# A graph-network layer on one core: layer two one group later, messages two groups further ahead

## The chip, the core and the metric

The kernel runs on one core of a Trainium2 chip, in a single launch. The metric is device time in microseconds; the time of the kernel before is 476.75 us, the median of three runs (476.61 to 477.19). TensorE (PE) does the matrix products and the transposes, VectorE (DVE) and ScalarE (ACT) the elementwise work, GpSimd (POOL) issues the gathers, SyncE (SP) all other transfers.

## The reference, cut to what matters

```python
# x (50000, 128); src, dst (25000,), dst sorted; edge_attr (25000, 128); W1 (128, 256); W2 (256, 128)
msg = relu(x[src] + edge_attr)
agg = segment_sum(msg, dst, num_segments=50000)
h = x + agg
h = relu(relu(h @ W1 + b1) @ W2 + b2)
out = layernorm(x + h)            # over the 128 features, no scale, no shift
```

## The kernel before

**Tiling.** The 50000 nodes are cut into 98 groups: 97 of 512 nodes (T = 4 tiles of 128) and a last one of 336. The edges are sorted by target, so the edges of a group lie in three windows of 128 edges, each for a third of its nodes (K = 3).

**What a group takes.** SP loads its x (`x_sb`) and its three windows of edge_attr (`pre_msg`); POOL gathers x[src] (`x_src`), three indirect transfers. DVE adds the two (`add_edge_attr`, L568). ACT takes the relu rounded to a short form, `msg_hi` (`high_part`, L718), and DVE what the rounding left, `msg_lo` (`low_part`, L575). DVE also writes `sel`, a matrix of ones and zeros that says which edge belongs to which node (`select`, L551). PE turns x (`turn_x`, L812, four transposes) and adds the messages on top in the same PSUM bank (`sum_messages`, L834, six products); ACT copies that to `hT` (`copy_hT`, L724). Layer one is `hidden_sum` on PE (L859, two products of 128x512) and `hidden` on ACT (L730, bias and relu into `h1T`); layer two is `output_sum` on PE (L867, eight products). DVE adds the bias (`add_bias`, L589), takes the relu and adds x (`add_x`, L601), and computes mean and variance (L608, L617); ACT takes the root (`deviation`, L735), DVE the reciprocal and the shift (L623, L628), ACT scales the four tiles (`normalize`, L749), SP stores.

**What sets the order.** The order on every engine is written out by hand, and each engine runs its own list strictly in order, waiting on semaphores. In the steady part, iteration g holds:
- PE: hidden_sum(g), turn_x(g+1), sum_messages(g+1), output_sum(g)
- ACT: hidden(g), deviation(g-2), copy_hT(g+1), normalize(g-3) with high_part(g+2) in its middle
- DVE: add_bias(g), low_part(g+2), add_x(g), reciprocal(g-2), statistics(g), shifts(g-2), select(g+3), aggregate(g), add_edge_attr(g+3)
- SP: x of group g+5, edge_attr of group g+5, the store of group g-4
- POOL: the gathers of group g, once `hT` of group g-3 is copied (GATHER_AHEAD = 3)

PSUM has eight banks: one for `hT_ps`, two for layer one (`h1T_ps`), two for layer two (`h2_ps`), two of the preparation (`prep_ps`) and a spare one. After group 3 the preparation's banks hold only one thing more, the sum of some flags (`sums_ps`, in `prep_ps[0]`), which say whether the windows are wide enough for the data. `sum_flags` writes it on PE in iteration CHECKED = 30, and `set_general` (L312) reads it on DVE at the end of iteration 31.

Of the kernel before, what the change touches and what calls it, by code (L numbers as in the profile page):

```python
# [8 lines left out]
ACT = mybir.ActivationFunctionType  # L9
AX_X = mybir.AxisListType.X  # L10
# [5 lines left out]
T = 4  # L16
# [17 lines left out]
ROWS = 125  # L34
CHECKED = 30
FAR = float(1 << 20)


EB, XB, ZB, YB, SB = 6, 6, 6, 4, 4
X_FIRST, X_AHEAD = 2, 5  # L40
GATHER_AHEAD = 3
ACT_TILES = 1
EA_FIRST, EA_AHEAD = 2, 5

# [118 lines left out]
def prepare(nc, x, edge_attr, dst, pairs, w1, b1, w2, b2, c, sb, sem):  # L163
# [9 lines left out]
    prep_ps = c["prep_ps"]  # L173
# [135 lines left out]
    def set_general(dve):  # L309

        dve.wait_ge(flags_summed, 1)
        nc.vector.reduce_max(c["general"][:, :], sums_ps, AX_X)  # L312

# [101 lines left out]
def main_path(nc, x, pairs, edge_attr, out, c, sb, sem, checks):  # L415
# [22 lines left out]
    hT = sb("hT", [128, T, 128])  # L438
    h1T = sb("h1T", [128, HC, T, 128])
    h2 = sb("h2", [128, 2, T, D])  # L440
# [18 lines left out]
    h2_summed = sem("h2_summed")  # L459
    h2_ready = sem("h2_ready")  # L460
    z_ready = sem("z_ready")
    stats_ready = sem("stats_ready")
# [8 lines left out]
    last_y_pool_ready = sem("last_y_pool_ready")  # L471

    def inside(g):

        return 0 <= g < GROUPS

    def main_sync(sp):
# [68 lines left out]
    def main_vector(dve):  # L546
# [8 lines left out]
        def edge_attr_there(g):  # L555

            dve.wait_ge(ea_loaded[g % EB], loads_to(g % EB, g, 0, c))
# [52 lines left out]

        def aggregate(g):
            p = partitions(g, c)
            dve.wait_ge(stats_ready, g + 1)
            for t in range(tiles(g, c)):
                if t == 1 and g >= 1 and inside(g + 3):
                    edge_attr_there(g + 3)
                last = nc.vector.bn_aggr(mean_var[0:p, g % SB, t, :], stats[0:p, g % SB, t, :])  # L617
            last.then_inc(var_ready, 1)
# [49 lines left out]
        statistics(1)  # L668
        select(4)
        aggregate(1)  # L670
        add_edge_attr(4)
        for g in range(2, LAST):
            add_bias(g)
            if inside(g + 2):
                low_part(g + 2)
            add_x(g)
            if inside(g - 2):
                reciprocal(g - 2)
            if g == LAST - 1:
                reciprocal(LAST - 2)  # L680
            statistics(g)
            if inside(g - 2):
                shifts(g - 2)
            if g == LAST - 1:
                shifts(LAST - 2)
            z_free(g + 1)
            if inside(g + 3):
                select(g + 3)
            aggregate(g)
            if inside(g + 3):  # L690
                add_edge_attr(g + 3)
            if g == CHECKED + 1:
                checks["set_general"](dve)
        add_bias(LAST)
# [13 lines left out]
    def main_scalar(act):  # L708
# [17 lines left out]
        def hidden(g, h):  # L726

            p, n = partitions(g, c), tiles(g, c)
            act.wait_ge(h1_summed, g * HC + h + 1)
            nc.scalar.activation(h1T[:, h, 0:n, 0:p], h1T_ps[h][:, 0:n, 0:p], ACT.Relu, bias=b1_sb[:, h:h + 1]).then_inc(h1_ready, 1)  # L730

# [43 lines left out]
        high_part(4)  # L775
        for g in range(3, LAST):
            for h in range(HC):
                hidden(g, h)
            if inside(g - 2):
                deviation(g - 2)  # L780
            if inside(g + 1):
                copy_hT(g + 1)
            for t in range(T):
                if inside(g - 3):
                    last = normalize(g - 3, t)
                if t == 1 and inside(g + 2):
                    high_part(g + 2)
            if inside(g - 3):
                last.then_inc(y_ready, 1)
        deviation(LAST - 2)  # L790
# [13 lines left out]
    def main_tensor(pe):  # L804
# [48 lines left out]
        def hidden_sum(g):  # L853
            p, n = partitions(g, c), tiles(g, c)
            pe.wait_ge(hT_copied, g + 1)
            for h in range(HC):
                if h == 1 and inside(g - 2):
                    pe.wait_ge(h2_ready, g - 1)
                nc.tensor.matmul(h1T_ps[h][:, 0:n, 0:p], w1_sb[:, h * 128:(h + 1) * 128], hT[:, 0:n, 0:p],  # L859
                                 start=True, stop=True).then_inc(h1_summed, 1)  # L860

        def output_sum(g, h):

            p = partitions(g, c)
            pe.wait_ge(h1_ready, g * HC + h + 1)
            for t in range(tiles(g, c)):
                last = nc.tensor.matmul(h2_ps[g % 2][0:p, t, :], h1T[:, h, t, 0:p], w2_sb[:, h, :],  # L867
                                        start=(h == 0 and t == 0), stop=(h == HC - 1), skip_group_check=True)
            if h == HC - 1:
                last.then_inc(h2_summed, 1)  # L870
# [31 lines left out]
        for g in (1, 2):  # L902
# [9 lines left out]
            output_sum(g, 1)  # L912
        for g in range(3, GROUPS):
            hidden_sum(g)
            if inside(g + 1):
                turn_x(g + 1)
                sum_messages(g + 1)
            if g == CHECKED:
                checks["sum_flags"](pe)
            for h in range(HC):  # L920
                output_sum(g, h)

# [370 lines left out]
```

## Time and profile before

| | |
|---|---|
| time, median of 3 runs | 476.75 us (476.61 to 477.19) |
| profiled execution, span from the first to the last instruction | 508.3 us |
| what the profile shows around that span | nothing that is timed |
| PE busy | 469.2 us (92%) |
| DVE busy | 409.9 us (81%) |
| ACT busy | 399.9 us (79%) |
| POOL busy | 320.8 us (63%) |
| mean granted TensorE clock | 0.991 of full speed |
| moved by DMA | 90.89 MB, 179 GB/s on average |

The profiled execution is 31.6 us longer than the median of the runs. A busy engine in the table is one that an instruction occupies; for PE the ends are modelled, so the start of the next row tells more than the length of a row. A wait that ends on "issue" or "remote" is one whose releaser the profile does not show.

### The profile page before, as it was taken

Reading aid. Unit: us, or ns where it says so; the run is one execution under the profiler, and the core shown is the slowest. Engines: PE = TensorE matmul, PEld = TensorE weight load, DVE = VectorE, ACT = ScalarE, POOL = GpSimd, SP = SyncE. Lnnn points to the kernel's source line nnn. Section 1 sums busy time; section 2 is a strip of 40 time slices with the busy share of each in tenths; the row PEclk is TensorE's granted clock in tenths of the full one; section 3 lists DMA queues with packets and bytes.
Section 4 is the critical chain, followed back from the end, with each engine's and each line's share of the span. In section 5 each row is a group of like instructions: output and inputs, shape, how many; then the busy total and the mean of one; then the engine's idle time right before and its main releaser. Section 6 shows DMA issues by size and latency. Waiting matters only on the chain.

```text
span 508.3 us, 9923 instructions
## 1 busy us (share of the span) xinstructions
PE 469.2 (92%) x2959; PEld 360.2 (71%) x2959; DVE 409.9 (81%) x1539; ACT 399.9 (79%) x881; POOL 320.8 (63%) x315
## 2 busy tenths in 40 slices
PE   5879999999989999989998989989899989989994
PEld 3647777676776777767786767767677867767773
DVE  6567879788797887977887877878778878878885
ACT  2328988797888898877887877878778878878885
POOL 7566766666756676666766656656566666666713
PEclk9979999999999999999999999999999999999999
DMA  5644656655656566655666656657556666656613
GB/s 134 168 135 155 193 185 201 196 175 184 195 173 190 183 206 203 177 174 177 195 199 181 192 173 184 186 172 204 170 183 186 202 182 182 203 173 188 218 58 117
DMA packets 81930, 90.89 MB, mean 179 GB/s; under 512 B 13841, under 2 KB 52372, under 8 KB 81876
## 3 DMA queue, kind: packets, MB, share of 16 engines
q1 hardware_dynamic: 71874, 70.80, 43.3%
q0 software_dynamic: 9728, 19.46, 16.6%
q8 instruction: 23, 0.38, 0.3%
q14 instruction: 31, 0.25, 0.1%
q10 hardware_dynamic: 274, 0.00, 0.0%
HBM read 64.61 MB, written 25.60 MB: 177 GB/s over the span
## 4 chain that ended last, share of the span: by engine, by line
PE 87%; issue 5%; ACT 3%; DVE 2%; another core or an unknown queue 2%; DMA 1%; POOL 0%; SPq 0%; DVEq 0%
PE h_ps L867 33%; PE h1T_ps L859 32%; PE hT_ps L834 13%; PE hT_ps L812 8%; ACT h1T L730 1%; ACT y L749 1%; ACT hT L724 1%; DMA dst_next<-in_dst_dram 1%; ACT msg_hi L718 0%; DVE stats L608 0%; DVE z L601 0%; DVE h L589 0%; DVE before_in_row L288 0%; DVE row_holds L358 0%
## 5 line engine op out<-in xcount | busy, mean ns | idle before, releaser
L109 POOL DMA_INDIRECT x_src<-in_x_dram,src_of x287 | 306.5, 1068 | 165.7 <-ACT hT L724 91.6
L867 PE MATMUL h_ps<-w_sb,h1T 128*128 128x128 f32 x1564 | 195.3, 278 | 3.2 <-ACT h1T L730 3.1
L867 PEld LDWEIGHTS h_ps<-w_sb,h1T 128*128 128x128 f32 x1564 | 183.7, 193 | 5.0 <-ACT h1T L730 4.9
L859 PE MATMUL h1T_ps<-hT,w_sb 128*128 128x512 f32 x392 | 185.7, 596 | 1.6 <-ACT hT L724 1.1
L730 ACT ACTIVATE h1T<-h1T_ps,b_sb 128x512 f32<-128x512 f32 x196 | 128.8, 680 | 55.6 <-PE h1T_ps L859 30.8
L749 ACT ACTIVATE y<-z,shift,rstd 128x128 f32<-128x128 f32 x382 | 165.6, 481 | 1.4 <-DVE shift L628 1.3
L589 DVE TENSOR_TENSOR h<-h_ps,b_sb 128x512 f32<-128x512 f32 x98 | 67.4, 688 | 81.9 <-remote 37.6
L859 PEld LDWEIGHTS h1T_ps<-hT,w_sb 128*128 128x128 f32 x392 | 67.5, 192 | 49.3 <-issue 47.7
L834 PE MATMUL hT_ps<-sel,msg_hi 128*128 128x168 f32 (+1 forms) x281 | 72.9, 293 | 20.8 <-issue 20.8
L608 DVE BATCH_NORM_STATS2 stats<-z 128x6 f32<-128x128 f32 x391 | 85.3, 281 | 0.0
L812 PEld LDWEIGHTS hT_ps<-ident,x_sb 128*128 128x128 f32 (+1 forms) x375 | 46.9, 141 | 50.0 <-issue 49.6
L724 ACT ACTIVATE hT<-hT_ps 128x512 f32<-128x512 f32 (+1 forms) x95 | 56.5, 595 | 21.5 <-PE hT_ps L834 17.5
L834 PEld LDWEIGHTS hT_ps<-sel,msg_hi 128*128 128x128 f32 x281 | 53.7, 191 | 26.3 <-issue 26.3
L834 PE MATMUL hT_ps<-sel,msg_lo 128*128 128x168 f32 (+1 forms) x281 | 67.4, 275 | 0.0
L601 DVE SCALAR_TENSOR_TENSOR z<-h,x_sb 128x512 f32<-128x512 f32 x98 | 66.8, 682 | 0.1
L551 DVE TENSOR_TENSOR sel<-node_in_range,dst_of 128x528 fp32r<-128x528 f32 x95 | 66.6, 701 | 0.0
L718 ACT ACTIVATE msg_hi<-pre_msg 128x384 fp32r<-128x384 f32 (+1 forms) x99 | 50.9, 514 | 17.5 <-issue 14.0
L575 DVE SCALAR_TENSOR_TENSOR msg_lo<-pre_msg,msg_hi 128x384 fp32r<-128x384 f32 (+1 forms) x99 | 54.0, 546 | 3.3 <-ACT msg_hi L718 2.2
L812 PE MATMUL hT_ps<-ident,x_sb 128*128 128x128 f32 (+1 forms) x375 | 56.3, 272 | 0.0
L568 DVE TENSOR_TENSOR pre_msg<-pre_msg,x_src 128x384 f32<-128x384 f32 (+2 forms) x101 | 51.7, 512 | 4.6 <-issue 2.9
L834 PEld LDWEIGHTS hT_ps<-sel,msg_lo 128*128 128x128 f32 x281 | 53.9, 192 | 0.0
L617 DVE BATCH_NORM_AGGREGATE mean_var<-stats 128x2 f32<-128x6 f32 x391 | 36.4, 155 | 0.1
(115 smaller groups left out, 121.2 us busy)
## 6 DMA issues: line engine op xcount, KB each, us to landing
x_sb<-in_x_dram SPq DMA_DIRECT2D x97, 256.0 KB
out_dram<-y SPq DMA_DIRECT2D x97, 256.0 KB
pre_msg<-in_edge_attr_dram SPq DMA_DIRECT2D x292, 64.0 KB
x_src<-in_x_dram,src_of POOLq DMA_INDIRECT x287
w_sb<-in_w_dram SPq DMA_DIRECT2D x2, 128.0 KB
x_sb<-in_x_dram SPq DMA_DIRECT2D x1, 168.0 KB
out_dram<-y SPq DMA_DIRECT2D x1, 168.0 KB
dst_rows<-in_dst_dram SPq DMA_DIRECT2D x1, 97.7 KB
```

The costliest lines, as they stand in the source:

```text
L109: nc.gpsimd.indirect_dma_start(out=c["x_src"][:, g % EB, k, :], out_offset=None, in_=x, in_offset=bass.IndirectOffsetOnAxis(ap=c["src_of"] ...
L551: nc.vector.tensor_tensor(sel[:, g % EB, 0:n, 0:width], in_range[:, :, :].to_broadcast([128, n, width]), dst_of[:, g:g + 1, 0:n].rearrange ...
L589: nc.vector.tensor_tensor(h2[0:p, g % 2, 0:n, :], h2_ps[g % 2][0:p, 0:n, :], b2_sb[0:p, :, :].to_broadcast([p, n, D]), ALU.add).then_inc(h ...
L601: nc.vector.scalar_tensor_tensor(z[0:p, g % ZB, 0:n, :], h2[0:p, g % 2, 0:n, :], 0.0, x_sb[0:p, g % XB, 0:n, :], ALU.max, ALU.add).then_in ...
L608: last = nc.vector.bn_stats(stats[0:p, g % SB, t, :], z[0:p, g % ZB, t, :])
L724: nc.scalar.activation(hT[:, 0:n, 0:p], sum_bank(g)[:, 0:n, 0:p], ACT.Copy).then_inc(hT_copied, 1)
L730: nc.scalar.activation(h1T[:, h, 0:n, 0:p], h1T_ps[h][:, 0:n, 0:p], ACT.Relu, bias=b1_sb[:, h:h + 1]).then_inc(h1_ready, 1)
L749: return nc.scalar.activation(y[0:p, g % YB, t, :], z[0:p, g % ZB, t, :], ACT.Identity, bias=shift[0:p, g % SB, t:t + 1], scale=rstd[0:p, ...
L812: nc.tensor.matmul(sum_bank(g)[:, t, 0:p], x_sb[0:p, g % XB, t, :], ident[0:p, 0:p], is_transpose=True, start=(t == 0), stop=False, skip_g ...
L834: last = nc.tensor.matmul(sum_bank(g)[:, 0:n, p0:p1], part[:, g % EB, k, :], cols, start=False, stop=final, skip_group_check=True)
L859: nc.tensor.matmul(h1T_ps[h][:, 0:n, 0:p], w1_sb[:, h * 128:(h + 1) * 128], hT[:, 0:n, 0:p], start=True, stop=True).then_inc(h1_summed, 1)
L867: last = nc.tensor.matmul(h2_ps[g % 2][0:p, t, :], h1T[:, h, t, 0:p], w2_sb[:, h, :], start=(h == 0 and t == 0), stop=(h == HC - 1), skip_ ...
```

## The change

Three things are moved, each by a constant or by the written order.

**PE and ACT.** From group LAG + 1 = 7 to UNLAG = 92, iteration g of PE does output_sum(g-1) in the place of output_sum(g). Iteration 6 has no output_sum, iteration 92 has two. `h1T` gets a second buffer, and layer one of every second group from 7 on writes to the two banks of the preparation (`hidden_bank`). For these banks to be free, the flags are summed in iteration 4 in place of 30 (CHECKED), and PE waits for set_general, a new semaphore, ahead of hidden_sum(7). On ACT, copy_hT(g+1) comes ahead of hidden(g), and deviation and normalize are of one group further back; at group 92 the old order returns, with one more deviation and one more normalize.

**DVE.** At group 6 DVE does low_part(8), select(9), add_edge_attr(9), select(10), low_part(9) and add_edge_attr(10) in one go. From there iteration g does select(g+5), low_part(g+4) and add_edge_attr(g+5) in the place of g+3, g+2 and g+3.

**Buffers and queues.** The buffers of messages, gathers and selections go from 6 to 8, those of x from 6 to 7. POOL's gathers of group g wait for hT of group g-5. SP loads edge_attr 6 groups ahead.

```diff
@@ -32,15 +32,18 @@
 LW = max(LP0[k + 1] - LP0[k] for k in range(LK))
 
 ROWS = 125
-CHECKED = 30
+CHECKED = 4
 FAR = float(1 << 20)
 
 
-EB, XB, ZB, YB, SB = 6, 6, 6, 4, 4
+EB, XB, ZB, YB, SB = 8, 7, 6, 4, 4
 X_FIRST, X_AHEAD = 2, 5
-GATHER_AHEAD = 3
+GATHER_AHEAD = 5
 ACT_TILES = 1
-EA_FIRST, EA_AHEAD = 2, 5
+EA_FIRST, EA_AHEAD = 2, 6
+
+LAG = 6
+UNLAG_BACK = 5
 
 FIRST_CHUNKS = 5
 SECOND = {1: (0, P0[1]), 2: (0, 128), 3: (0, 128), 4: (P0[2], 128)}
@@ -309,7 +312,7 @@
     def set_general(dve):
 
         dve.wait_ge(flags_summed, 1)
-        nc.vector.reduce_max(c["general"][:, :], sums_ps, AX_X)
+        return nc.vector.reduce_max(c["general"][:, :], sums_ps, AX_X)
 
     def find_ends(pe):
 
@@ -436,7 +439,7 @@
     msg_lo = sb("msg_lo", [128, EB, K, D], FP32R)
     msg_whole = sb("msg_whole", [128, len(WHOLE), D])
     hT = sb("hT", [128, T, 128])
-    h1T = sb("h1T", [128, HC, T, 128])
+    h1T = sb("h1T", [128, 2, HC, T, 128])
     h2 = sb("h2", [128, 2, T, D])
     z = sb("z", [128, ZB, T, D])
     y = sb("y", [128, YB, T, D])
@@ -458,6 +461,7 @@
     h1_ready = sem("h1_ready")
     h2_summed = sem("h2_summed")
     h2_ready = sem("h2_ready")
+    general_set = sem("general_set")
     z_ready = sem("z_ready")
     stats_ready = sem("stats_ready")
     var_ready = sem("var_ready")
@@ -470,9 +474,15 @@
     last_y_dve_ready = sem("last_y_dve_ready")
     last_y_pool_ready = sem("last_y_pool_ready")
 
+    UNLAG = LAST - UNLAG_BACK
+
     def inside(g):
 
         return 0 <= g < GROUPS
+
+    def hidden_bank(g, h):
+
+        return c["prep_ps"][h].rearrange("p (t n) -> p t n", t=T) if g > LAG and (g - LAG) % 2 else h1T_ps[h]
 
     def main_sync(sp):
         def load_x(g):
@@ -608,12 +618,12 @@
                 last = nc.vector.bn_stats(stats[0:p, g % SB, t, :], z[0:p, g % ZB, t, :])
             last.then_inc(stats_ready, 1)
 
-        def aggregate(g):
+        def aggregate(g, ahead=None):
             p = partitions(g, c)
             dve.wait_ge(stats_ready, g + 1)
             for t in range(tiles(g, c)):
-                if t == 1 and g >= 1 and inside(g + 3):
-                    edge_attr_there(g + 3)
+                if t == 1 and ahead is not None and inside(ahead):
+                    edge_attr_there(ahead)
                 last = nc.vector.bn_aggr(mean_var[0:p, g % SB, t, :], stats[0:p, g % SB, t, :])
             last.then_inc(var_ready, 1)
 
@@ -667,11 +677,25 @@
         add_x(1)
         statistics(1)
         select(4)
-        aggregate(1)
+        aggregate(1, 4)
         add_edge_attr(4)
         for g in range(2, LAST):
+            if g == LAG:
+                low_part(g + 2)
+                select(g + 3)
+                edge_attr_there(g + 3)
+                add_edge_attr(g + 3)
+                select(g + 4)
+                low_part(g + 3)
+                edge_attr_there(g + 4)
+                add_edge_attr(g + 4)
+            lagged = g >= LAG
+            ahead = g + (5 if lagged else 3)
             add_bias(g)
-            if inside(g + 2):
+            if lagged:
+                if inside(ahead):
+                    select(ahead)
+            else:
                 low_part(g + 2)
             add_x(g)
             if inside(g - 2):
@@ -684,13 +708,15 @@
             if g == LAST - 1:
                 shifts(LAST - 2)
             z_free(g + 1)
-            if inside(g + 3):
-                select(g + 3)
-            aggregate(g)
-            if inside(g + 3):
-                add_edge_attr(g + 3)
+            if not lagged:
+                select(ahead)
+            elif inside(g + 4):
+                low_part(g + 4)
+            aggregate(g, ahead)
+            if inside(ahead):
+                add_edge_attr(ahead)
             if g == CHECKED + 1:
-                checks["set_general"](dve)
+                checks["set_general"](dve).then_inc(general_set, 1)
         add_bias(LAST)
         add_x(LAST)
         reciprocal(LAST - 1)
@@ -727,7 +753,7 @@
 
             p, n = partitions(g, c), tiles(g, c)
             act.wait_ge(h1_summed, g * HC + h + 1)
-            nc.scalar.activation(h1T[:, h, 0:n, 0:p], h1T_ps[h][:, 0:n, 0:p], ACT.Relu, bias=b1_sb[:, h:h + 1]).then_inc(h1_ready, 1)
+            nc.scalar.activation(h1T[:, g % 2, h, 0:n, 0:p], hidden_bank(g, h)[:, 0:n, 0:p], ACT.Relu, bias=b1_sb[:, h:h + 1]).then_inc(h1_ready, 1)
 
         def deviation(g):
             p, n = partitions(g, c), tiles(g, c)
@@ -773,20 +799,45 @@
         deviation(0)
         copy_hT(3)
         high_part(4)
-        for g in range(3, LAST):
+        def normalize_all(g, between=None):
+            for t in range(T):
+                last = normalize(g, t)
+                if t == 1 and between is not None and inside(between):
+                    high_part(between)
+            last.then_inc(y_ready, 1)
+
+        for g in range(3, LAG):
             for h in range(HC):
                 hidden(g, h)
-            if inside(g - 2):
-                deviation(g - 2)
-            if inside(g + 1):
-                copy_hT(g + 1)
-            for t in range(T):
-                if inside(g - 3):
-                    last = normalize(g - 3, t)
-                if t == 1 and inside(g + 2):
-                    high_part(g + 2)
+            deviation(g - 2)
+            copy_hT(g + 1)
             if inside(g - 3):
-                last.then_inc(y_ready, 1)
+                normalize_all(g - 3, g + 2)
+            else:
+                high_part(g + 2)
+        copy_hT(LAG + 1)
+        high_part(LAG + 2)
+        for h in range(HC):
+            hidden(LAG, h)
+        high_part(LAG + 3)
+        for g in range(LAG + 1, UNLAG):
+            copy_hT(g + 1)
+            for h in range(HC):
+                hidden(g, h)
+            deviation(g - 3)
+            normalize_all(g - 4, g + 3)
+        for g in range(UNLAG, LAST):
+            for h in range(HC):
+                hidden(g, h)
+            if g == UNLAG:
+                deviation(g - 3)
+            deviation(g - 2)
+            copy_hT(g + 1)
+            if g == UNLAG:
+                normalize_all(g - 4)
+            if inside(g + 3):
+                high_part(g + 3)
+            normalize_all(g - 3)
         deviation(LAST - 2)
         for h in range(HC):
             hidden(LAST, h)
@@ -855,8 +906,8 @@
             pe.wait_ge(hT_copied, g + 1)
             for h in range(HC):
                 if h == 1 and inside(g - 2):
-                    pe.wait_ge(h2_ready, g - 1)
-                nc.tensor.matmul(h1T_ps[h][:, 0:n, 0:p], w1_sb[:, h * 128:(h + 1) * 128], hT[:, 0:n, 0:p],
+                    pe.wait_ge(h2_ready, g - 2 if LAG < g <= UNLAG else g - 1)
+                nc.tensor.matmul(hidden_bank(g, h)[:, 0:n, 0:p], w1_sb[:, h * 128:(h + 1) * 128], hT[:, 0:n, 0:p],
                                  start=True, stop=True).then_inc(h1_summed, 1)
 
         def output_sum(g, h):
@@ -864,7 +915,7 @@
             p = partitions(g, c)
             pe.wait_ge(h1_ready, g * HC + h + 1)
             for t in range(tiles(g, c)):
-                last = nc.tensor.matmul(h2_ps[g % 2][0:p, t, :], h1T[:, h, t, 0:p], w2_sb[:, h, :],
+                last = nc.tensor.matmul(h2_ps[g % 2][0:p, t, :], h1T[:, g % 2, h, t, 0:p], w2_sb[:, h, :],
                                         start=(h == 0 and t == 0), stop=(h == HC - 1), skip_group_check=True)
             if h == HC - 1:
                 last.then_inc(h2_summed, 1)
@@ -911,14 +962,22 @@
             sum_messages(g + 1)
             output_sum(g, 1)
         for g in range(3, GROUPS):
+            if g == LAG + 1:
+                pe.wait_ge(general_set, 1)
             hidden_sum(g)
             if inside(g + 1):
                 turn_x(g + 1)
                 sum_messages(g + 1)
             if g == CHECKED:
                 checks["sum_flags"](pe)
-            for h in range(HC):
-                output_sum(g, h)
+            if LAG < g <= UNLAG:
+                for h in range(HC):
+                    output_sum(g - 1, h)
+            if g == UNLAG:
+                pe.wait_ge(h2_ready, g - 1)
+            if g < LAG or g >= UNLAG:
+                for h in range(HC):
+                    output_sum(g, h)
 
     return dict(sync=main_sync, gpsimd=main_gpsimd, vector=main_vector, scalar=main_scalar, tensor=main_tensor)
```

The instructions of PE where the two orders part; `h1T_ps0` and `prep_ps0` are banks of layer one, `h2_ps` of layer two. Before, the end of iteration 6 and the head of iteration 7:

```order
L834 MATMUL hT_ps<-sel,msg_lo 128x4x42
L867 MATMUL h2_ps0<-w2_sb,h1T 128x128 [waits h1_ready]
L867 MATMUL h2_ps0<-w2_sb,h1T 128x128 x3
L867 MATMUL h2_ps0<-w2_sb,h1T 128x128 [waits h1_ready]
L867 MATMUL h2_ps0<-w2_sb,h1T 128x128 x3
L859 MATMUL h1T_ps0<-hT,w1_sb 128x512 [waits hT_copied]
L859 MATMUL h1T_ps1<-hT,w1_sb 128x512 [waits h2_ready]
```

The same place of PE in the changed kernel:

```order
L885 MATMUL hT_ps<-sel,msg_hi 128x4x42
L885 MATMUL hT_ps<-sel,msg_lo 128x4x42
L910 MATMUL prep_ps0<-hT,w1_sb 128x512 [waits hT_copied,general_set]
L910 MATMUL prep_ps1<-hT,w1_sb 128x512 [waits h2_ready]
L863 MATMUL hT_ps<-ident,x_sb 128x128 [waits x_loaded1]
```

The eight products of layer two of group 6 have gone from here to the end of iteration 7, and hidden_sum(7) waits for one semaphore more.

DVE at the end of iteration 5 and the head of iteration 6, before:

```order
L568 TENSOR_TENSOR pre_msg<-pre_msg,x_src 128x384 [waits xsrc_loaded2]
L589 TENSOR_TENSOR h2<-h2_ps0,b2_sb 128x512 [waits h2_summed]
L575 SCALAR_TENSOR_TENSOR msg_lo<-pre_msg,msg_hi 128x384 [waits msg_hi_ready]
L601 SCALAR_TENSOR_TENSOR z<-h2,x_sb 128x512 [waits h2_ready]
L623 RECIPROCAL rstd<-std 128x4 [waits std_ready]
```

The same place of DVE in the changed kernel:

```order
L578 TENSOR_TENSOR pre_msg<-pre_msg,x_src 128x384 [waits xsrc_loaded0]
L315 TENSOR_REDUCE general<-prep_ps0 1x1 [waits flags_summed]
L585 SCALAR_TENSOR_TENSOR msg_lo<-pre_msg,msg_hi 128x384 [waits msg_hi_ready]
L561 TENSOR_TENSOR sel<-node_in_range,dst_of 128x528
L578 TENSOR_TENSOR pre_msg<-pre_msg,x_src 128x384 [waits xsrc_loaded1,ea_loaded1]
L561 TENSOR_TENSOR sel<-node_in_range,dst_of 128x528
L585 SCALAR_TENSOR_TENSOR msg_lo<-pre_msg,msg_hi 128x384 [waits msg_hi_ready]
L578 TENSOR_TENSOR pre_msg<-pre_msg,x_src 128x384 [waits xsrc_loaded2,ea_loaded2]
L599 TENSOR_TENSOR h2<-h2_ps0,b2_sb 128x512 [waits h2_summed]
L561 TENSOR_TENSOR sel<-node_in_range,dst_of 128x528
```

The reduction that PE waits for stands behind the whole of iteration 5, and the work that brings DVE two groups ahead stands between it and the bias of group 6.

ACT in iteration 6 before, a round of the steady part:

```order
L730 ACTIVATE h1T<-h1T_ps0,b1_sb 128x512 [waits h1_summed]
L730 ACTIVATE h1T<-h1T_ps1,b1_sb 128x512 [waits h1_summed]
L735 ACTIVATE std<-mean_var,eps_col 128x4 [waits var_ready]
L724 ACTIVATE hT<-hT_ps 128x512 [waits hT_summed]
L749 ACTIVATE y<-z,shift,rstd 128x128 [waits shift_ready]
L749 ACTIVATE y<-z,shift,rstd 128x128
L718 ACTIVATE msg_hi<-pre_msg 128x384 [waits sum_ready]
```

ACT in iteration 7 of the changed kernel, the first such round in the new order:

```order
L750 ACTIVATE hT<-hT_ps 128x512 [waits hT_summed]
L756 ACTIVATE h1T<-prep_ps0,b1_sb 128x512 [waits h1_summed]
L756 ACTIVATE h1T<-prep_ps1,b1_sb 128x512 [waits h1_summed]
L761 ACTIVATE std<-mean_var,eps_col 128x4 [waits var_ready]
L775 ACTIVATE y<-z,shift,rstd 128x128 [waits shift_ready]
L775 ACTIVATE y<-z,shift,rstd 128x128
L744 ACTIVATE msg_hi<-pre_msg 128x384 [waits sum_ready]
```

The copy of the next group's `hT` has moved ahead of the relu of this group's layer one.

## Rows read from the trace of the kernel before

**Rows 1.** The chain that ended last: shares of the span by engine.
```profile
PE 87%; issue 5%; ACT 3%; DVE 2%; another core or an unknown queue 2%; DMA 1%; POOL 0%; SPq 0%; DVEq 0%
```
**Rows 2.** Timeline of PE: start us, us, engine line op out<-in xcount [idle before <-releaser].
```profile
252.29 1.88 PE L859 MATMUL h1T_ps<-hT,w_sb 128*128 128x512 f32 x4
...
254.37 0.33 PE L834 MATMUL hT_ps<-sel,msg_hi 128*128 128x176 f32 x1
...
255.09 1.98 PE L867 MATMUL h_ps<-w_sb,h1T 128*128 128x128 f32 x16
256.90 0.59 PE L859 MATMUL h1T_ps<-hT,w_sb 128*128 128x512 f32 x1
```
**Rows 3.** Timeline of DVE, the same stretch.
```profile
252.52 0.68 DVE L589 TENSOR_TENSOR h<-h_ps,b_sb 128x512 f32<-128x512 f32 x1
253.19 0.56 DVE L575 SCALAR_TENSOR_TENSOR msg_lo<-pre_msg,msg_hi 128x384 fp32r<-128x384 f32 x1
253.66 0.68 DVE L601 SCALAR_TENSOR_TENSOR z<-h,x_sb 128x512 f32<-128x512 f32 x1
...
255.17 0.14 DVE L628 SCALAR_TENSOR_TENSOR shift<-mean_var,rstd 128x4 f32<-128x4 f32 x1
255.23 0.70 DVE L551 TENSOR_TENSOR sel<-node_in_range,dst_of 128x528 fp32r<-128x528 f32 x1
255.85 0.37 DVE L617 BATCH_NORM_AGGREGATE mean_var<-stats 128x2 f32<-128x6 f32 x4
256.14 0.52 DVE L568 TENSOR_TENSOR pre_msg<-pre_msg,x_src 128x384 f32<-128x384 f32 x1
```
**Rows 4.** Timeline of ACT, the same stretch.
```profile
252.63 0.53 ACT L718 ACTIVATE msg_hi<-pre_msg 128x384 fp32r<-128x384 f32 x1 [0.47 <-issue]
253.06 0.86 ACT L749 ACTIVATE y<-z,shift,rstd 128x128 f32<-128x128 f32 x2
253.83 1.24 ACT L730 ACTIVATE h1T<-h1T_ps,b_sb 128x512 f32<-128x512 f32 x2
254.97 0.29 ACT L735 ACTIVATE std<-mean_var,eps_col 128x4 f32<-128x4 f32 x1
255.29 0.60 ACT L724 ACTIVATE hT<-hT_ps 128x512 f32<-128x512 f32 x1
255.78 0.87 ACT L749 ACTIVATE y<-z,shift,rstd 128x128 f32<-128x128 f32 x2
```
**Rows 5.** Waits of PE: total us, times, longest us.
```profile
PE hT_ps L834 <- issue: 20.8, 23, 1.4
```
**Rows 6.** Timeline of PE, one pause.
```profile
222.48 0.60 PE L812 MATMUL hT_ps<-ident,x_sb 128*128 128x128 f32 x4
224.49 0.35 PE L834 MATMUL hT_ps<-sel,msg_hi 128*128 128x176 f32 x1 [1.41 <-issue]
```
**Rows 7.** Timeline of DVE, the same pause.
```profile
220.00 0.53 DVE L568 TENSOR_TENSOR pre_msg<-pre_msg,x_src 128x384 f32<-128x384 f32 x1
223.28 0.69 DVE L589 TENSOR_TENSOR h<-h_ps,b_sb 128x512 f32<-128x512 f32 x1 [2.76 <-issue]
```
**Rows 8.** Timeline of PE: layer one of group 4 and of group 96.
```profile
41.92 1.88 PE L859 MATMUL h1T_ps<-hT,w_sb 128*128 128x512 f32 x4
...
494.25 1.88 PE L859 MATMUL h1T_ps<-hT,w_sb 128*128 128x512 f32 x4
```
**Rows 9.** Timeline of groups 2 and 3, PE and ACT.
```profile
30.60 1.16 PE L867 MATMUL h_ps<-w_sb,h1T 128*128 128x128 f32 x8 [2.01 <-ACT h1T L730]
...
35.02 0.60 ACT L724 ACTIVATE hT<-prep_ps 128x512 f32<-128x512 f32 x1 [3.41 <-remote]
...
35.67 3.52 PE L859 MATMUL h1T_ps<-hT,w_sb 128*128 128x512 f32 x4 [1.09 <-ACT hT L724]
```
**Rows 10.** Busy times of 20 to 40 us: length, PE, PEld, DVE, ACT, POOL, granted clock, DMA.
```profile
20.00:40.00 20.00, 16.44 (x81) 11.59 (x79) 13.97 (x48) 6.95 (x15) 13.46 (x13) 0.83 0.57 168
```
**Rows 11.** The reduction of the flags on DVE: duration in ns, start.
```profile
L312 DVE TENSOR_REDUCE general<-prep_ps x1: 147/147/147, 182.9 to 182.9; 1x1 int32<-1x9 f32 x1
```
**Rows 12.** Timeline of POOL, two gathers of one group.
```profile
252.98 0.94 POOL L109 DMA_INDIRECT x_src<-in_x_dram,src_of  x1 [0.30 <-issue]
254.23 0.95 POOL L109 DMA_INDIRECT x_src<-in_x_dram,src_of  x1 [0.30 <-issue]
```

## The prediction

> **What bounds the kernel now.** I read the chain of waits first: PE holds 87% of it [rows 1]. Then the timeline of PE over one group, to see how full it is. H(g) is the start of hidden_sum(g) below. From one H to the next it is 256.90 - 252.29 = 4.61 us [rows 2]: sum_messages begins at H + 2.08, output_sum at H + 2.80, the next group at H + 4.61, and no row in between has idle time ahead of it. So in such a group PE has nothing left to wait for, and what the change may win must come from groups that are longer.
>
> These exist in the profiled execution. From H(4) at 41.92 to H(96) at 494.25 [rows 8] there are 92 groups, 452.3 us, where 92 x 4.61 makes 424.1. That leaves 28.2 us. The waits of PE show them as 23 pauses ahead of sum_messages [rows 5]. One of them: the transposes begin at 222.48, the first message product at 224.49, 2.01 us later where 0.36 would do [rows 2, 6]. DVE says why: it had nothing to do from 220.53 on and began add_bias only at 223.28, after 2.76 us of idle time [rows 7], though by PE's rows output_sum had ended long before. PE's signal came late, low_part stood behind add_bias, and PE waited for low_part.
>
> Are these pauses in the timed runs? The profiled execution takes 508.3 us (nothing that is timed lies around its span), the runs 476.75: 31.6 less. The pauses make 28.2, a further one ahead of 30.60 makes 2.0 [rows 9], and hidden_sum(3) ran in 3.52 us where others take 1.88 [rows 2, 9], since the granted clock was 0.83 in that stretch, so at 1.2 GHz for a part of it [rows 10]: 1.6. Together 31.8. So I take it that the timed runs have next to none of them. How much could they have? ACT idled another 3.41 us before the copy of group 3 [rows 9], also for a late signal; if that too belongs to the profiled execution alone, 5 us or so of the timed runs are unexplained, and may be pauses or something around the span. Bounds for what the change can win back: 0 and 5 us. I take 0, since the sum closes.
>
> The Trainium skill, page "Runtime: NRT & Kernel Launch", section "The ~15µs preamble/postamble breakdown", says that a profile's total is about 6.2 us above the executed time, whatever the kernel. Here the gap is 31.6, so the trace does not agree. By that rule the other 25.4 us would be pauses of the profiled execution, and 28.2 - 25.4 = 2.8 of them would be in the timed runs too: by it the change ends at no difference.
>
> **The change part by part.**
>
> *The steady part, groups 8 to 91.* PE has the same 20 products a group in another order: 4.61 us, nothing saved while it is full. Does a new wait come in? ACT's steps from start to start are high_part 0.43, two normalizes 0.77, two hiddens 1.14, deviation 0.32, copy to the next 0.49, two normalizes 0.77 [rows 4]: 3.92 us a group, below 4.61. It now begins its round with copy_hT(g+1), which can start at about H + 3.0 and is done at H + 3.6, 1.0 us before PE wants it, as now (255.29 + 0.60 against 256.90 [rows 2, 4]). The round ends at H + 6.9, before the next copy at H + 7.6. DVE takes 256.14 + 0.52 - 252.52 = 4.14 us [rows 3], below 4.61. low_part(g+2) is done now at 253.75 for products at 254.37 [rows 2, 3]: 0.6 us of slack. In the new order low_part is ready about 3 us earlier relative to its products, so a late signal of 2 us would be covered. That is the gain, and it needs pauses to act on. Cost here 0; bounds -5 (above) and +1 (should ACT or DVE now and then be late).
>
> *SP and POOL.* SP's store(g-4) now waits for a normalize that comes one iteration later, and the loads of x and edge_attr stand behind it in SP's queue; they are 5 and 6 groups ahead, some 20 us, so the 4.61 us that this costs are hidden. POOL issues a gather each 254.23 - 252.98 = 1.25 us [rows 12], 3.75 a group, less than PE's 4.61, and is freed two groups earlier. 0.
>
> *Group 6 to 7, where the lag begins.* Count from H(6) = 0. Iteration 6 has no output_sum, so PE is done at 2.80. Then it waits for general_set. DVE's iteration 5 starts at 0.23 (252.52 against 252.29), its last add begins 3.62 later and takes 0.52 [rows 2, 3], the reduction 0.15 [rows 11], the signal about 0.1: 4.6. PE idles 4.6 - 2.8 = 1.8 us. Without general_set it would still wait for copy_hT(7), at 2.8 + 0.2 + 0.6 = 3.6: 0.8. Bounds: 0.8, and 3.0 if DVE has to wait for the gathers of group 8, a gather's 1.25 us. I take 1.8. Behind the waiting hidden_sum(7) everything on PE is queued; its lost time is not made up, since PE is full afterwards. DVE's extra work (two low_parts, two selects, two adds; 0.47, 0.62 and 0.52 each [rows 3], 3.2 us) ends near 7.9, and output_sum(6) ends at 9.2, so DVE is in time for add_bias(6). The messages of group 9 are wanted at 11.3 and ready near 7.7. 0.
>
> *Group 92, where it ends.* Count from H(92) = 0. ACT ends its round at 2.3, does hidden(92) and deviation(89) to 3.8, waits for the variance of group 90 until 0.23 + (255.85 + 0.37 - 252.52) = 3.9 [rows 3] and copies hT(93) by 4.9; PE wants it at 6.42, after two output_sums. DVE's iteration 91 begins at 4.84. There select stands ahead of the shift and low_part behind it, so the shift takes 2.65 + 0.62 - 0.47 = 2.80 after its start [rows 3] and is there at 7.8. ACT's four extra normalizes run from there to 7.8 + 1.54 = 9.3, then hidden(93, 0) in 0.68 to 10.0. PE wants that at 6.42 + 2.80 = 9.22. PE idles 0.8 us. One group later ACT ends at 13.4 what PE wants relued by 14.7: no further wait. Bounds: 0, and 1.9 for all the extra work of that round (1.54 + 0.32 [rows 4]).
>
> *The tail.* The same order as now from group 93 on, with DVE less loaded (no select and no add left). 0.
>
> Sum: 1.8 + 0.8 + 0 = 2.6 us. Forecast 476.75 + 2.6 = 479.35 us, about 0.5% slower. The profiled execution, whose pauses it covers, should fall to between 480 and 492 us all the same.
>
> **The rivals.**
>
> *Faster: the timed runs have the late signals too.* With the upper bound of 5 us in pauses, all covered, the time is 476.75 + 2.6 - 5 = 474.3. For it: the pauses come at regular distances and in 23 places, and the lag has just the slack that they need. Against it: the sum of 31.8 against 31.6 leaves nothing for the timed runs.
>
> *No change: about half of that.* 2 to 3 us of pauses are covered and pay for the two gaps: 476.75 + 2.6 - 2.5 = 476.85. For it: the unexplained part of the head is of this size.
>
> *Much slower: the gap of 1.8 us makes the clock fall.* In the head the granted clock fell after PE had idled 2.0 us ahead of 30.60 [rows 9, 10]. 0.17 of 20 us is 3.4 us of lost clock, so 476.75 + 2.6 + 3.4 = 482.75. Against it: the pauses of 2 us between 42 and 494 us left the clock at full speed, for hidden_sum takes 1.88 us at both ends [rows 8]. The Trainium skill, page "TensorE: Matmul & The Clock Gate", section "What's actually happening", says that an idle TensorE goes back to 1.2 GHz; by it a gap is dangerous here, though the trace shows one such fall only.
>
> **How the numbers follow.** Chances: forecast 0.56, faster rival 0.24, no change 0.16, clock 0.04. The forecast's own range is 476.75 + 0.8 to 476.75 + 4.9, so 477.5 to 481.7. To leave out no more than 2 in 10 the range goes from 474.0, just below the faster rival, to 482.0. A difference of 0.2% (1 us) is about what a measurement of this kernel can tell from none. Slower: 0.56 + 0.04 = 0.60. Same: 0.16. Faster: 0.24.
>
> **What the new profile would show.** Right: PE idle 1 to 3 us before the first L910 that writes `prep_ps`, released by the reduction on DVE; groups at 4.61 us; few or no pauses ahead of the message products, though DVE and ACT still get late signals; one wait of PE under 2 us near group 93; 14 us or more off the span while the timed median hardly moves. Wrong: a timed median that falls as the span does (then the pauses are in the timed runs as well); groups above 4.61 us with PE waiting for `hT` or `h1T` (ACT has become the bound); new waits of DVE on gathers or edge_attr in the head.

## The result, and the profile after

The changed kernel takes 479.29 us (median of 4 runs, 478.47 to 480.66), the kernel before 476.68 us beside it: a ratio of 1.0066, with a 95% interval of 1.0051 to 1.0082. It is slower by 2.6 us, as forecast (479.35), and its two gaps are where the prediction put them. The ratios here and below leave out slow runs, so they aren't the quotients of the medians beside them.

Its trace has no pause like those of [rows 6, 7], and its time is 1.8 us above its span (479.47 and 477.7 us). In every run here the time is 1.7 to 2.1 us above the span, so something that is timed does lie around it.

```profile
core 0: 477.7 us, clock 0.994
```

The first gap, on PE (start, duration, engine, line, operation, in brackets the idle time before and its releaser):

```profile
45.95 1.88 PE L910 MATMUL h1T_ps<-hT,w_sb 128*128 128x512 f32 x4
...
48.63 0.28 PE L885 MATMUL hT_ps<-sel,msg_lo 128*128 128x168 f32 x1
50.35 1.98 PE L910 MATMUL prep_ps<-hT,w_sb 128*128 128x512 f32 x4 [1.44 <-DVE general L315]
```

and on DVE, the same stretch:

```profile
46.15 0.69 DVE L599 TENSOR_TENSOR h<-h_ps,b_sb 128x512 f32<-128x512 f32 x1 [0.50 <-PE h_ps L918]
...
49.70 0.52 DVE L578 TENSOR_TENSOR pre_msg<-pre_msg,x_src 128x384 f32<-128x384 f32 x1
50.15 0.15 DVE L315 TENSOR_REDUCE general<-prep_ps 1x1 int32<-1x9 f32 x1
```

H(6) is at 45.95. PE's work of iteration 6 is 2.80 us [rows 2], so it is free at 48.75 and starts again at 50.35: 1.6 us lost. The clock did not fall: in the row of 50 to 60 us the granted clock, third from the end, is 1.00.

```profile
50.00:60.00 10.00, 9.65 (x61) 7.51 (x62) 7.97 (x24) 8.02 (x18) 7.76 (x8) 1.00 0.45 126
```

The second gap, PE and then ACT:

```profile
448.91 1.88 PE L910 MATMUL prep_ps<-hT,w_sb 128*128 128x512 f32 x4
450.63 0.60 PE L863 MATMUL hT_ps<-ident,x_sb 128*128 128x128 f32 x4
450.99 0.33 PE L885 MATMUL hT_ps<-sel,msg_hi 128*128 128x176 f32 x1
...
452.51 2.05 PE L918 MATMUL h_ps<-w_sb,h1T 128*128 128x128 f32 x16 [0.64 <-ACT h1T L756]
454.40 1.88 PE L910 MATMUL h1T_ps<-hT,w_sb 128*128 128x512 f32 x4
```

```profile
450.24 1.65 ACT L775 ACTIVATE y<-z,shift,rstd 128x128 f32<-128x128 f32 x4 [1.09 <-DVE shift L638]
451.79 1.24 ACT L756 ACTIVATE h1T<-prep_ps,b_sb 128x512 f32<-128x512 f32 x2
```

From H(93) to H(94) it is 454.40 - 448.91 = 5.49 us where 4.61 would do: 0.9 us. ACT waited for the shift, did four normalizes, and only then the relu that PE stood for. Between the gaps the groups are 4.61 us long (the first, from H(7) to H(8), 4.71), and what ACT waits for most is PE's sum:

```profile
ACT hT L750 <- PE hT_ps L885: 65.0, 90, 2.0
```

### The profile page after: what moved, and what is told of

The parts are those of the page before. It is cut to its first block, busy times and chain, and to the rows that moved or that the text cites. A ratio compares the mean times of both kernels' runs of the same rounds, so it can differ in the third digit from the quotient of the medians.

```text
span 477.7 us, 10016 instructions
## 1 busy us (share of the span) xinstructions
PE 460.7 (96%) x2959; PEld 359.3 (75%) x2959; DVE 412.7 (86%) x1539; ACT 381.7 (80%) x881; POOL 322.6 (68%) x315
## 4 chain that ended last, share of the span: by engine, by line
PE 90%; DVE 4%; DMA 3%; POOL 1%; ACT 1%; issue 1%; ACTq 0%; DVEq 0%
PE h_ps L918 36%; PE h1T_ps L910 17%; PE prep_ps L910 16%; PE hT_ps L885 12%; PE hT_ps L863 8%; DMA x_src<-in_x_dram,src_of 1%; DMA x_src<-in_x_dram,first_pairs 1%; DVE stats L618 1%; DVE h L599 1%; DVE z L611 1%; POOL x_src L112 1%; DMA first_pairs<-in_pairs_dram 1%; PE hT_ps L892 0%; DVE pre_msg L578 0%; DVE sel L561 0%
## 5 line engine op out<-in xcount | busy, mean ns | idle before, releaser
L910 PE MATMUL h1T_ps<-hT,w_sb 128*128 128x512 f32 x208 | 98.0, 594 | 0.0
L910 PE MATMUL prep_ps<-hT,w_sb 128*128 128x512 f32 (+1 forms) x184 | 86.1, 590 | 1.4 <-DVE general L315 1.4
L756 ACT ACTIVATE h1T<-h1T_ps,b_sb 128x512 f32<-128x512 f32 x104 | 66.1, 685 | 4.4 <-PE h1T_ps L910 4.4
L561 DVE TENSOR_TENSOR sel<-node_in_range,dst_of 128x528 fp32r<-128x528 f32 x95 | 68.9, 725 | 0.0
L756 ACT ACTIVATE h1T<-prep_ps,b_sb 128x512 f32<-128x512 f32 (+1 forms) x92 | 57.9, 682 | 0.6 <-PE prep_ps L910 0.6
L910 PEld LDWEIGHTS h1T_ps<-hT,w_sb 128*128 128x128 f32 x208 | 35.7, 191 | 24.9 <-issue 24.9
```

What stands on the lines that cost most here:

```text
L561: nc.vector.tensor_tensor(sel[:, g % EB, 0:n, 0:width], in_range[:, :, :].to_broadcast([128, n, width]), dst_of[:, g:g + 1, 0:n].rearrange ...
L756: nc.scalar.activation(h1T[:, g % 2, h, 0:n, 0:p], hidden_bank(g, h)[:, 0:n, 0:p], ACT.Relu, bias=b1_sb[:, h:h + 1]).then_inc(h1_ready, 1)
L910: nc.tensor.matmul(hidden_bank(g, h)[:, 0:n, 0:p], w1_sb[:, h * 128:(h + 1) * 128], hT[:, 0:n, 0:p], start=True, stop=True).then_inc(h1_su ...
```

## The experiments

The jobs ran on different chips, and that matters. The runs of the kernel before took 509 us on one chip, 527 on a second, and 476.1 and 475.8 on the two of the last jobs. The first two are called disturbed below, the others quiet. Each chip was used in one job only, so whether it is the chip or its state at that time stays open. Times are compared within a job only.

**b_again** (no edit), disturbed.

> The kernel before, unchanged, profiled and timed once more. Theory: the 23 pauses of PE ahead of the message products belong to one profiled execution and not to the kernel; the timed runs' own spans lie near 475 us, and a further profile either lies there too, with groups at 4.61 us throughout, or has pauses that its timed runs don't have. Rival (the pauses are in the timed runs too): the spans of the timed runs are well above what 92 groups of 4.61 us, the head and the tail make, and every one has pauses.

Measured: 509.4 us, ratio to before 1.003 (0.999 to 1.007); the timed runs' own spans are 504 to 513 us. In its trace:

```profile
DVE h L589 <- remote: 41.1, 14, 6.6
PE hT_ps L834 <- issue: 16.3, 21, 1.3
```

A span of 504 us or more has room for such pauses and none near 475 us has, so they are in the timed runs of this chip. My theory that a profiled execution alone has them is refuted. The trace shown ahead of the prediction (508.3 us) is of this kind, while the median beside it, 476.75, is of the other. The record doesn't say on which chip that trace was taken.

**b_quiet** (no edit, one run), quiet.

> The kernel before, unchanged, for a profile on a chip without late signals, should this be one. Theory: groups at 4.61 us from group 4 or 5 to 96 with no pause, span near 474.3; its head up to H(6) equals that of the changed kernel within some tenths. Rival: pauses here too, or a head that is a microsecond or more shorter than that of the changed kernel, so that the prefetch has a price in the head.

Measured: 475.94 us, span 474.1. Layer one of group 5 and of group 96, and between them the sum of the flags in iteration 30:

```profile
39.96 1.02 PE L859 MATMUL h1T_ps<-hT,w_sb 128*128 128x512 f32 x2
```

```profile
158.16 0.20 PE L322 MATMUL prep_ps<-violations,ones_col 128*1 128x9 f32 x2
```

```profile
459.99 1.02 PE L859 MATMUL h1T_ps<-hT,w_sb 128*128 128x512 f32 x2
```

That is 420.03 us for 91 groups. Iteration 30 takes 4.90 us because PE sums the flags in it (in the changed kernel, iteration 4 takes 4.90 us for the same reason); the other 90 take 4.61 each. So there is no pause, and nothing for a lag to win.

H(6) is at 44.58 here and at 45.95 in the changed kernel's trace, so by its number the rival's head, a microsecond shorter, is there. It is not the price of the deeper queues: best_2 and best_lag20 below have the same queues and their H(6) at 44.61 and 43.77. The start of the head varies in one and the same kernel: H(0) is at 13.45 here and at 14.26 in b_again, and at 14.78 in the changed kernel.

**a_flags3** and **flags3_2**: the flags one iteration earlier.

```diff
-CHECKED = 4
+CHECKED = 3
```

> The changed kernel with CHECKED = 3, so that set_general stands behind iteration 4 of DVE and no longer behind iteration 5. Theory: the wait of PE ahead of hidden_sum(7) falls from 1.6 us to the 0.8 us of the copy of hT(7), 0.7 us less in all: 478.6 where the changed kernel has 479.3. Rival (the wait was hidden or is taken over by low_part(8) or another one): 479.3, with a new wait in group 7 or 8.

> The changed kernel with CHECKED = 3: set_general behind iteration 4 of DVE. On a quiet chip, theory: the wait ahead of hidden_sum(7) falls from 1.6 to 0.8 us, the time by 0.7 us against the changed kernel in this job (478.6 for 479.3). Rival (something takes its place): no difference, a new wait in group 7 or 8. On a chip with pauses it can't be told apart by its time, only in the trace at H(7).

Both jobs were disturbed: 515.6 us where before took 508.9 (ratio 1.018, 1.011 to 1.024), and 523.1 beside 523.7 of the changed kernel (ratio to before 0.997, 0.994 to 1.001). The times decide nothing about a gap of 0.7 us. The trace of the second does, for this place:

```profile
63.72 0.28 PE L885 MATMUL hT_ps<-sel,msg_lo 128*128 128x168 f32 x1
64.77 0.67 PE L910 MATMUL prep_ps<-hT,w_sb 128*128 128x512 f32 x1 [0.78 <-ACT hT L750]
```

The reduction no longer ends the wait; the copy of `hT` does, and H(7) is 3.73 us behind H(6) (61.04): 0.9 us lost in place of 1.6.

**a_spread** and **spread_2**: ACT's extra normalizes in iteration 94.

```diff
-            if g == UNLAG:
+            if g <= UNLAG + 2:
                 normalize_all(g - 4)
             if inside(g + 3):
                 high_part(g + 3)
-            normalize_all(g - 3)
+            if g >= UNLAG + 2:
+                normalize_all(g - 3)
```

> The changed kernel with the extra group of normalizes on ACT moved from iteration 92 to iteration 94. Theory: the 0.8 us that PE waits for h1T in iteration 93 goes, and iteration 95 has no wait in its place: 478.5. Rival (the wait only moves, since ACT has too little room up to the end): 479.3, with a wait for h1T in iteration 95 or a longer tail.

> The changed kernel with the extra group of normalizes on ACT moved from iteration 92 to 94. On a quiet chip, theory: the 0.9 us ahead of output_sum(93) go, nothing in their place: 478.5 for 479.3. Rival: the wait moves to iteration 95 or into the tail: 479.3.

Disturbed both times: 514.0 us beside before's 508.9 (1.014, 1.008 to 1.020), and 522.2 beside the changed kernel's 523.7 (ratio to before 0.996, 0.992 to 1.000). In the second trace iteration 93 has no gap, products of messages and of layer two following at once:

```profile
496.80 0.33 PE L886 MATMUL hT_ps<-sel,msg_hi 128*128 128x176 f32 x1
...
497.52 0.75 PE L919 MATMUL h_ps<-w_sb,h1T 128*128 128x128 f32 x5
```

There are 0.72 us between them, as in a full group [rows 2]. The rival is right in part: a short wait stands in iteration 95 instead, where the last product of messages begins at 506.64 and output_sum at 506.94, behind the relu of ACT.

```profile
506.64 0.27 PE L886 MATMUL hT_ps<-sel,msg_lo 128*128 128x168 f32 x1
506.94 2.05 PE L919 MATMUL h_ps<-w_sb,h1T 128*128 128x128 f32 x16
```

```profile
506.21 1.24 ACT L756 ACTIVATE h1T<-prep_ps,b_sb 128x512 f32<-128x512 f32 x2
```

From H(95) to H(96) it is 4.87 us, so 0.3 of the 0.9 us are moved there. In a_spread's trace it is 4.88 us.

**after_2**: the changed kernel, disturbed.

> The changed kernel unchanged, beside the kernel before on whatever chip this job gets. On the chip of the last job every run of the kernel before took some 509 us, with pauses of PE behind late signals; on the chip of the first result it took 476.7. Theory now: the pauses belong to the chip or its state, not to profiling and not to the kernel. If this chip is quiet (before near 477): 479.3, two gaps of 1.6 and 0.9 us. If it has the pauses: the lag doesn't pay here either, since a late signal then meets the copy of hT, which has 1.0 us of slack; 512 to 516 against 509. Rival (the lag covers the pauses): below 500 on such a chip.

Measured: 523.7 us, before 527.1, ratio 0.998 (0.994 to 1.002). The lag doesn't remove the late signals' effect but moves a part of it: the copy of `hT` now waits for them. From 62 to 490 us, behind the head:

```profile
DVE h L599 <- remote: 75.2, 22, 5.1
ACT hT L750 <- remote: 41.5, 20, 2.5
PE prep_ps L910 <- ACT hT L750: 6.2, 13, 1.5
PE h1T_ps L910 <- ACT hT L750: 5.0, 13, 0.5
```

DVE waits for its signal as before, and PE waits 26 times for the copy. In the head one signal costs as much as these 26 together: hidden_sum(3) waited 11.5 us for its copy, ahead of where the lag begins. In all that is no difference of 2% either way, and far above the 500 us below which the lag would have absorbed the pauses.

On the other disturbed chip, that of the first job, the versions with a lag took 1.4 and 1.8% more than before (a_spread, a_flags3), on this one up to 0.5% less. What makes the sign differ was not found.

**best_1** and **best_2**: both mends, and the lag begun in halves.

```diff
+            if g == LAG:
+                output_sum(g, 0)
             if LAG < g <= UNLAG:
                 for h in range(HC):
-                    output_sum(g - 1, h)
+                    if g > LAG + 1 or h == 1:
+                        output_sum(g - 1, h)
```

On ACT, hidden(6, 0), copy_hT(7), hidden(6, 1) stand in this order, with high_part(8) and high_part(9) behind.

> CHECKED = 3, the normalizes spread, and the lag begun in two steps: iteration 6 does the first half of output_sum(6), iteration 7 the second, and ACT does hidden(6, 0) ahead of the copy of hT(7) and hidden(6, 1) behind it. Theory: no gap of PE is left at either place, and the time is that of before, 476.7 (within 0.5 us), but not below it, because PE is full in both. Rival (the deeper prefetch costs or brings something of its own): 477.5 and above, or 476 and below.

> The version with all three mends (flags one iteration earlier, normalizes spread, lag begun in two halves), once more beside the kernel before, in the hope of a chip without late signals. In the last job its trace had no gap at H(7) and one of 0.2 us in iteration 95. Theory on a quiet chip: 476.7 + 0.2, within 0.5 us of before. Rival (the prefetch has a price of its own in the head): 477.5 or above. On a chip with late signals: 0 to 4 us below before, and nothing is settled.

The first job was disturbed (521.4 us, before 527.1; ratio 0.995, 0.992 to 0.998), so there this version was a little faster, as expected for such a chip. The second was quiet: 478.18 us beside 476.11, ratio 1.0045 (1.0032 to 1.0059). So 2.1 us are still lost although both gaps are mended. The trace of the quiet run says where. PE, DVE, ACT:

```profile
51.22 1.08 PE L919 MATMUL h_ps<-w_sb,h1T 128*128 128x128 f32 x8
53.72 1.98 PE L911 MATMUL h1T_ps<-hT,w_sb 128*128 128x512 f32 x4 [1.41 <-ACT hT L750]
```

```profile
52.06 0.56 DVE L578 TENSOR_TENSOR pre_msg<-pre_msg,x_src 128x384 f32<-128x384 f32 x1 [1.41 <-DMA x_src<-in_x_dram,src_of]
...
55.83 0.56 DVE L578 TENSOR_TENSOR pre_msg<-pre_msg,x_src 128x384 f32<-128x384 f32 x1 [2.06 <-DMA x_src<-in_x_dram,src_of]
```

```profile
52.66 0.52 ACT L744 ACTIVATE msg_hi<-pre_msg 128x384 fp32r<-128x384 f32 x1 [3.21 <-DVE pre_msg L578]
53.09 0.58 ACT L750 ACTIVATE hT<-hT_ps 128x512 f32<-128x512 f32 x1
```

DVE asks at group 6 for the gathers of groups 9 and 10, which have not landed. ACT stands in high_part(9), the copy of hT(8) behind it, and PE behind that. H(8) comes 5.37 us after H(7) (48.35), where this iteration holds half an output_sum, 3.70 us of work: 1.67 us lost. Iteration 95 has 4.88 us and loses another 0.3.

Why were the gathers late? The last one of group 9 is the 24th of this kind. In the changed kernel and in best_2:

```profile
47.56 1.16 POOL L112 DMA_INDIRECT x_src<-in_x_dram,src_of  x1 [0.30 <-issue]
```

```profile
49.28 0.95 POOL L112 DMA_INDIRECT x_src<-in_x_dram,src_of  x1 [0.30 <-issue]
```

The 13 gathers ahead of it took 1.31 us each in the changed kernel's trace and 1.47 in this one, where [rows 12] has 1.25. So in the changed kernel's trace group 9 came in time, and only the gathers of group 10 were late. Had they been as late as here, the gap at general_set would have hidden it: H(8) is 9.11 us behind H(6) in both traces. The trace of best_1, the same kernel as best_2, has long pauses in its head; there DVE's adds of groups 9 and 10 (66.33 and 67.94) have no idle time ahead of them, and H(8) is 3.91 us behind H(7).

**a_ahead** and **ahead_2**: DVE's half of the change alone. PE and ACT keep the old order, and high_part(g+3) stands right behind hidden(g).

```diff
-            if g == LAG + 1:
-                pe.wait_ge(general_set, 1)
...
-            if LAG < g <= UNLAG:
-                for h in range(HC):
-                    output_sum(g - 1, h)
...
-            if g < LAG or g >= UNLAG:
-                for h in range(HC):
-                    output_sum(g, h)
+            for h in range(HC):
+                output_sum(g, h)
```

> Only one half of the change: DVE two groups further ahead, with the new buffers and queues; PE and ACT in the order of before (output_sum(g) in iteration g, no wait for general_set), ACT's high_part(g+3) right behind hidden(g). Theory: both gaps belong to the lag, so PE has none here: 476.7, within 0.5 us of before. Rival (part of the 2.6 us is the price of the deeper prefetch in the head or of DVE's catching up at group 6): 477.2 to 478.5, with PE waiting for msg_lo or hT after group 6.

> Only DVE's half of the change: messages two groups further ahead, PE and ACT without the lag, high_part(g+3) right behind hidden(g). It was 36 us above before on a chip with late signals, where PE waited for h1T: ACT's relu of layer one gates output_sum(g) in the same iteration, and low_part waits for high_part. Theory on a quiet chip: no late signal, so 476.7 to 478. Rival (this order of ACT and DVE is slower by itself, ACT being the bound): 485 or more there too, with groups above 4.61 us without any late signal.

Disturbed: 545.3 us beside 508.9 (1.075, 1.067 to 1.082), refuting the 476.7 to 478.5 of both theories there. Quiet: 480.34 beside 476.11, 1.0074 (1.0055 to 1.0092), which is above the theory's 476.7 to 478 and below the rival's 485. Its groups are 4.61 us long from H(9) on, so ACT isn't the bound; in the trace, whose run took 481.75 us, 6.0 us are lost between H(7) and H(9):

```profile
54.34 3.17 PE L899 MATMUL h_ps<-w_sb,h1T 128*128 128x128 f32 x16 [1.96 <-ACT h1T L756]
58.12 3.78 PE L891 MATMUL h1T_ps<-hT,w_sb 128*128 128x512 f32 x4 [0.61 <-ACT hT L750]
```

The same gathers are late here: DVE waited 1.7 us for those of group 9 and 2.0 for those of group 10, ACT stood in high_part, and PE behind ACT. A lower clock followed. After 1.96 us of idle time the granted clock was 1.00 up to 55 us and 0.50 from there to 61, the lower of its two levels, 1.2 GHz, so hidden_sum took 3.78 us where a full clock gives 1.88. The row of 50 to 60 us, with its mean of 0.75:

```profile
50.00:60.00 10.00, 7.42 (x33) 5.17 (x32) 6.27 (x16) 3.62 (x9) 7.87 (x8) 0.75 0.40 104
```

**best_lag20**: as best_2, with the lag begun at group 20.

```diff
-LAG = 6
+LAG = 20
```

> The version with all three mends, and the lag begun at group 20 and not at 6. In the last job, without late signals, the mended version had lost its gap at H(7), but PE idled 1.4 us ahead of H(8): the gathers of group 9 landed late, since POOL issues them back to back at 1.25 us and DVE asked for two groups more at once; ACT stood in high_part(9) with the copy of hT(8) behind it. Theory: POOL gains 0.6 to 0.8 us a group on PE, so by group 20 it is two groups ahead, no gap is left there, and the time is within 0.3 us of before (476.1). Rival (the lag or the deeper buffers cost something by themselves): still 1 us or more above before.

Measured: 476.53 us beside 475.76, ratio 1.0018 (1.0008 to 1.0029). So the 1.67 us are gone, and what is left is 0.8 us, above the 0.3 expected and below the rival's 1. PE where the lag begins:

```profile
108.34 1.88 PE L911 MATMUL h1T_ps<-hT,w_sb 128*128 128x512 f32 x4
111.14 1.09 PE L919 MATMUL h_ps<-w_sb,h1T 128*128 128x128 f32 x8
112.08 1.96 PE L911 MATMUL prep_ps<-hT,w_sb 128*128 128x512 f32 x4
114.95 1.09 PE L919 MATMUL h_ps<-w_sb,h1T 128*128 128x128 f32 x8
115.95 1.98 PE L911 MATMUL h1T_ps<-hT,w_sb 128*128 128x512 f32 x4
...
120.66 1.88 PE L911 MATMUL prep_ps<-hT,w_sb 128*128 128x512 f32 x4
```

From 108.34 to 120.66 it is 12.32 us for 12.0 of work, and iteration 95 has 4.87 us for 4.61. That makes 0.3 + 0.3 of the 0.8. The last 0.2 us are open; they are within the interval. It is the best of the versions with a lag that were measured on a quiet chip, and none of these is faster than the kernel before.

## Why the prediction was right

**What bounds.** Right. PE is full at 4.61 us a group, in the timed runs of a quiet chip as in the undisturbed groups of the trace. The kernel before lost nothing in 91 groups of b_quiet but the 0.3 us of its flag sum.

**The pauses.** The conclusion (next to none in the timed runs of 476.7 us) is right, the reason wrong. I set the sum 28.2 + 2.0 + 1.6 = 31.8 against 31.6 and read it as the price of profiling. The runs refuted that reading: a disturbed chip has the pauses in its timed runs, and a quiet one has none in a profiled run. So trace and median come most likely from two chips, or from one in two states; the record doesn't name them. That the sum closed was luck. It set a span against a time, and times are some 1.8 us above spans: 508.3 against about 474.9 are 33.4 us. b_quiet's trace shows where they lie: up to H(4) it is 6.6 us shorter (35.35 against 41.92), where I had counted 3.6. My choice of 0 for the pauses, on which the whole forecast stands, came from this sum. The same error made the forecast of the new span, 480 to 492 us, too high: it was 477.7.

**Group 6 to 7.** Forecast 1.8 us, measured 1.6; without general_set 0.8, measured 0.9 (flags3_2). DVE's iteration was 0.2 us shorter than the sum: each instruction begins before the one ahead of it has ended, and the signal, for which I took 0.1 without a row, took 0.05 (the reduction ends at 50.30, H(7) is at 50.35). What I cost at nothing was DVE's catching up: I had the gathers of groups 9 and 10 landed in time, since POOL takes 3.75 us a group at its best. In the trace of best_2 it took 4.4, and they were 1.4 and 2.1 us late. In the changed kernel DVE waited 1.0 us for the second, one of my signs of being wrong, but without loss to PE. So this 0 was right for the change as it stands, and wrong once its first gap is mended.

**Group 92.** Forecast 0.8 us, measured 0.9, by the mechanism given: shift, four normalizes, relu. With the normalizes spread, best_2 has 4.61 us from H(93) to H(94) on a quiet chip.

**The steady part, the queues, the tail.** 0 forecast; the groups between the gaps are 4.61 us long. From H(4) to H(97) the changed kernel took 467.88 - 36.44 = 431.4 us, the kernel before 464.25 - 35.35 = 428.9 in b_quiet, a trace of another job: 2.5 us, of the 2.6 measured.

**The rivals.** Faster and no change needed pauses in the timed runs of the first result; the changed kernel's trace has none, and b_quiet's has none at the same time of 476 us. On a disturbed chip, where there are some, the changed kernel was no better than before: 0.998 in after_2. The claim that a lag has just the slack for a late signal fails, since the signal of hT_ps can be late too, and its copy has 1.0 us. The clock did not fall at the gap of 1.6 us, but did after 1.96 us of idle time in ahead_2. My argument against that rival was weaker than it looked: the pauses that I called 2 us long are 1.4 us of idle time at most [rows 5, 6], less than the 1.8 that I forecast for the gap. The nearest idle time above 1.8 was the 2.0 us of [rows 9], and after it the clock had fallen.

## What to carry to other kernels

When an engine is full, more slack for the engines around it wins nothing, and a change of order can cost a gap where it begins and where it ends; count these gaps first. When the profiled span and the timed median differ by more than a few us, ask first whether they are of one chip, and take a trace beside the timed runs. A sum that closes is no proof that its terms explain the difference. An edit that is hidden by a gap of the same change must be priced again when that gap is mended.

## What the runs showed that I had not expected

The same kernel takes 476, 509 or 527 us in jobs on different chips. On the disturbed ones DVE waits up to 6.6 us for one signal (b_again) whose sender, by its rows, has long been done. The long groups are partly the same in two traces of one kernel: those from H(43), H(46) and H(51) take 6.0, 5.1 and 6.3 us in the trace of [rows 6] and 6.2, 5.2 and 6.5 in that of b_again. What holds the signals back was not found. Such a chip can turn a difference of 4 us into one of 36 (ahead_2 against a_ahead).
